# The last pair of heads of a fused transformer kernel: gates from exponentials, output chunks finished inside the loop, the last chunk in halves

## The reference, cut to what matters

```python
xn = layernorm(x)
s = attention1(xn)      # 16 heads of 64, causal, relative positions;
                        # s = concat(heads) @ out_kernel + out_bias
f = sigmoid(xr @ W_r.T) * (square(relu(xk @ W_k.T)) @ W_v.T)
g = f * sigmoid(f)      # silu
out = x + s * g
```

## Time and profile before

| what | value |
|---|---|
| median of three runs | 1199.7 us |
| the profiled execution's own time | 1197.8 us |
| its span in the trace | 1196.1 us |
| PE busy | 1138.2 us (95% of the span) |
| POOL busy | 832.8 us (70%) |
| DVE busy | 819.7 us (69%) |
| ACT busy | 688.4 us (58%) |

### The profile page before, as it was taken

The page is one execution under the profiler, slowest core; times in us unless marked ns, Lnnn a source line. Parts: engine busy times, 40 slices in busy tenths (PEclk is TensorE's granted clock), DMA queues, the critical chain, the costliest instruction groups (busy, mean ns, idle before and its releaser), DMA issues.

```text
span 1196.1 us, 31475 instructions
## 1 busy us (share of the span) xinstructions
PE 1138.2 (95%) x11940; PEld 751.9 (63%) x11948; DVE 819.7 (69%) x2041; ACT 688.4 (58%) x1376; POOL 832.8 (70%) x1111
## 2 busy tenths in 40 slices
PE   4999999999979999999999999999999999999997
PEld 1344566678736666667666766666676666676665
DVE  4778878613776876786687578668668767866552
ACT  3543363357335666576566656666666665765665
POOL 0787432102444987978888798788879879788895
PEclk9999999999999999999999999999999999999998
DMA  8300010113034220302302031040212203023001
GB/s 309 138 1 1 1 45 19 48 51 93 23 70 87 70 46 14 83 6 46 79 21 46 20 81 32 16 90 11 46 44 57 46 17 80 6 46 81 2 3 37
DMA packets 74891, 60.19 MB, mean 50 GB/s; under 512 B 38962, under 2 KB 69298, under 8 KB 73652
## 3 DMA queue, kind: packets, MB, share of 16 engines
q1 hardware_dynamic: 73716, 56.08, 18.8%
q0 software_dynamic: 1024, 2.09, 0.6%
HBM read 19.76 MB, written 4.72 MB: 20 GB/s over the span
## 4 chain that ended last, share of the span: by engine, by line
PE 68%; ACT 2%; DVE 1%; issue 1%; DVEq 0%
PE S L1980 10%; PE S L1981 10%; PE S L1982 10%; PE A L1970 9%; PE O L1994 6%; PE O L1995 5%; PE O L1992 5%; PE M L1961 3%; PE M L1938 2%; PE M L1940 2%; PE M L1939 2%; PE M L1955 1%; PE M L1948 1%; PE M L1946 1%; PE M L1947 1%
## 5 line engine op out<-in xcount | busy, mean ns | idle before, releaser
L1722 POOL TENSOR_TENSOR plow<-prob 128x512 f16<-128x512 f32 (+3 forms) x640 | 588.5, 931 | 94.5 <-ACT prob L2198 70.4
L2198 ACT ACTIVATE prob<-S,keep_sigma 128x512 f32<-128x512 f32 (+3 forms) x640 | 396.1, 626 | 263.7 <-PE S L1982 260.8
L2299 DVE CUSTOM_DVE_ANT_0 junk<-A,mask_rows,part 128x512 bf16<-128x512 f32 (+3 forms) x384 | 248.9, 648 | 98.0 <-PE A L1970 76.8
L1992 PE MATMUL O<-V,prob 128*128 128x65 f16 x2176 | 232.7, 193 | 0.2 <-POOL plow L1722 0.2
L1994 PE MATMUL O<-V,prob 128*128 128x64 f16 x2176 | 232.5, 194 | 0.0
L1995 PE MATMUL O<-V,plow 128*128 128x65 f16 x2176 | 231.7, 192 | 0.0
L1980 PE MATMUL S<-rows 97*128 97x512 f16 (+3 forms) x640 | 223.1, 349 | 3.8 <-ACT prob L2198 3.5
L1981 PE MATMUL S<-rows 96*128 96x512 f16 (+3 forms) x640 | 222.3, 347 | 0.0
L1970 PE MATMUL A<-rows 96*128 96x512 f16 (+3 forms) x640 | 221.0, 346 | 1.3 <-DVE part L2299 1.0
L1982 PE MATMUL S<-rows 96*128 96x512 f16 (+3 forms) x640 | 220.7, 345 | 0.0
L1992 PEld LDWEIGHTS O<-V,prob 128*128 128x128 bf16 x2176 | 203.0, 97 | 23.6 <-POOL plow L1722 0.3
(11 more groups left out here) (388 smaller groups left out, 1845.3 us busy)
## 6 DMA issues: line engine op xcount, KB each, us to landing
rows<-stage_rows SPq DMA_DIRECT2D x64, 256.0 KB, 3.4
V<-stage_v SPq DMA_DIRECT2D x16, 516.0 KB, 4.6
W<-in_W SPq DMA_DIRECT2D x2, 2048.0 KB, 14.2
shifted<-turned SPq DMA_DIRECT2D x32, 128.0 KB, 2.2
rows<-stage_pos SPq DMA_DIRECT2D x64, 64.0 KB, 3.1
w<-in_w SPq DMA_DIRECT2D x2, 1024.0 KB, 10.6
xe_rows<-zero SPq DMA_DIRECT2D x1, 1280.0 KB, 5.3
ye_rows<-xe SPq DMA_DIRECT2D x5, 256.0 KB, 3.2
```

Source lines behind the costliest of these rows:

```text
L1722: pool.tensor_tensor(plow[:, k % PB, 0:w], full, full.bitcast(BF16).rearrange("p (q e) -> p q e", e=2)[:, :, 1], ALU.subtract).then_inc(s_ ...
L1992: pe.matmul(both, high[:, cs, 1], vh[h][:, j, 0:HS + 1], start=(j == 0 and s == 0), stop=False, skip_group_check=True)
L2198: act.activation(prob[:, k % PB, 0:w], S[k % 2][:, 0:w], ACT.Exp, scale=sigma[:, 2 * p + h:2 * p + h + 1]).then_inc(s_exp, 1)
L2299: dve.tensor_tensor_reduce(junk[:, g % 2, 0:w], A[g % 2][:, 0:w], add, -1.0, before, ALU.add, ALU.min, out).then_inc(s_max, 1)
```

## The change

The gates are no longer made by Silu. In slots 22 to 29 of the last pair ACT writes exp(-f) into `turned`, in eight pieces of 256 columns (`negated`). DVE makes f / (1 + exp(-f)) from it with three operations for each chunk (`opened`), in slots 56, 60, 62 and 64. It multiplies `acc` by the gate and adds the residual (`finish`) for chunk 0 in slot 66, chunk 1 in 68, chunk 3 (without its last projection) in 73, and chunk 2 in 79. In a slot `opened` and `finish` stand behind the items and ahead of `inverted`. The last chunk of the last head sums its upper two tiles in bank A0 in place of O1, and is inverted, scaled, transposed, projected, multiplied by its gate, added and stored in two halves.

```diff
--- before.py
+++ after.py
@@ -1689,7 +1689,12 @@
         bank.n, bank.of_bank = 0, [0, 0]
         for _ in range(base_n + 7 * PER + TAIL):
             bank.take()
-        fin_items = [("turn", 0, 3, bank.take()), ("project", 0, 3, bank.take())]
+        HALF = TPC // 2
+        fin_turn = [bank.take() for _ in range(2)]
+        fin_project = [bank.take() for _ in range(2)]
+        NEGATED = {22 + k: k for k in range(2 * NC)}
+        OPENED = {56 + 2 * c + 2 * (c > 0): c for c in range(NC)}
+        FINISHED = {66: 0, 68: 1, 73: 3, 79: 2}
 
         JOINS = [(c, step) for c in range(NC) for step in range(3)]
         PRO_A = NB - LEAD
@@ -1828,11 +1833,12 @@
                 pair(p, False)
 
             pair(PAIRS - 1, True)
-            for c in range(NC):
-                sp.wait_ge(s_fin, 2 * c + 2)
-                sp.dma_start(out_dram.rearrange("b (n p) d -> p (b n) d", p=P)[:, TPC * c:TPC * (c + 1), :],
-                             acc[:, TPC * c:TPC * (c + 1), :]).then_inc(s_out, 16)
-            sp.wait_ge(s_out, 16 * NC)
+            stored = out_dram.rearrange("b (n p) d -> p (b n) d", p=P)
+            for ready, t0, t1 in ((2, 0, TPC), (4, TPC, 2 * TPC), (8, 2 * TPC, 3 * TPC), (10, 3 * TPC, 3 * TPC + HALF),
+                                  (12, 3 * TPC + HALF, NT)):
+                sp.wait_ge(s_fin, ready)
+                sp.dma_start(stored[:, t0:t1, :], acc[:, t0:t1, :]).then_inc(s_out, 16)
+            sp.wait_ge(s_out, 16 * 5)
 
 
         @block.gpsimd
@@ -1984,12 +1990,14 @@
 
             def values(h, c, j, n):
                 r = max(0, j - TPC * c)
+                halved = n >= ALL - TPC * NC
                 high = prob[:, n % PB, :].bitcast(BF16).rearrange("p (q e) -> p q e", e=2)
                 for s in range(r, TPC):
                     cs = slice((s - r) * P, (s - r + 1) * P)
                     at = s * (HS + 1)
-                    both, part = O[c % 2][:, at:at + HS + 1], O[c % 2][:, at:at + HS]
-                    pe.matmul(both, high[:, cs, 1], vh[h][:, j, 0:HS + 1], start=(j == 0 and s == 0), stop=False,
+                    sums = A[0] if halved and s >= HALF else O[c % 2]
+                    both, part = sums[:, at:at + HS + 1], sums[:, at:at + HS]
+                    pe.matmul(both, high[:, cs, 1], vh[h][:, j, 0:HS + 1], start=(j == 0 and (s == 0 or halved and s == HALF)), stop=False,
                               skip_group_check=True)
                     pe.matmul(part, high[:, cs, 1], vh[h][:, j, HS + 1:VW], start=False, stop=False, skip_group_check=True)
                     ins = pe.matmul(both, plow[:, n % PB, cs], vh[h][:, j, 0:HS + 1], start=False, stop=j == TPC * c + s,
@@ -2089,6 +2097,8 @@
                 if j == 0:
                     if 2 * NC * p + NC * h + c >= 2:
                         pe.wait_ge(s_otok, 2 * NC * p + NC * h + c)
+                    if 2 * NC * p + NC * h + c == 2 * NC * PAIRS - 1:
+                        pe.wait_ge(s_max, PRO_A + PER_A * (PAIRS - 1) + LEAD + NB)
                     if c == 0:
                         pe.wait_ge(s_mv[h], 16 * (p + 1))
                 pe.wait_ge(s_low, SLOTS * p + m + 1)
@@ -2104,9 +2114,20 @@
                 for k in two:
                     if k >= DRAIN:
                         value_tile(*divmod(k - DRAIN, SLOTS))
-            for (kind, rel, c, tok) in fin_items:
-                item(kind, rel, c, (tok[0] - PER * (PAIRS - 1), tok[1], tok[2] - PER // 2 * (PAIRS - 1)), PAIRS - 1,
-                     turn_tok=(fin_items[0][3][0], fin_items[0][3][1], fin_items[0][3][2] - PER // 2 * (PAIRS - 1)))
+            for k in range(2):
+                _, b, used = fin_turn[k]
+                pe.wait_ge(s_free[b], used)
+                pe.wait_ge(s_otok, 2 * NC * PAIRS + 1 + k)
+                for i in range(HALF * k, HALF * (k + 1)):
+                    ins = pe.transpose(M[b][:, i * P:(i + 1) * P], otok[:, TPC * (NC - 1) + i, :], ident[:])
+                ins.then_inc(s_item, 1)
+            for k in range(2):
+                pe.wait_ge(s_free[fin_turn[k][1]], fin_turn[k][2] + 1)
+                _, b, used = fin_project[k]
+                pe.wait_ge(s_free[b], used)
+                for i in range(HALF * k, HALF * (k + 1)):
+                    ins = pe.matmul(M[b][:, i * P:(i + 1) * P], oT[:, i * P:(i + 1) * P], wo[:, PAIRS, :], start=True, stop=True)
+                ins.then_inc(s_item, 1)
 
 
         @block.scalar
@@ -2207,12 +2228,33 @@
                     act.wait_ge(s_item, count(turn_item(plan[p == PAIRS - 1], -1, 3), p)[0])
                 if g == 0:
                     act.wait_ge(s_otok, 1)
+                if g == 2 * NC * PAIRS - 1:
+                    for k in range(2):
+                        act.wait_ge(s_rec, g + 1 + k)
+                        scaled_tiles(h, c, (O[c % 2], A[0])[k], HALF * k, HALF * (k + 1))
+                        _, b, _ = fin_turn[k]
+                        act.wait_ge(s_item, fin_turn[k][0] + 1)
+                        at = slice(HALF * k * P, HALF * (k + 1) * P)
+                        act.activation(oT[:, at], M[b][:, at], ACT.Copy).then_inc(s_free[b], 1)
+                    return
                 act.wait_ge(s_rec, g + 1)
-                for s in range(TPC):
+                scaled_tiles(h, c, O[c % 2], 0, TPC)
+
+            def scaled_tiles(h, c, sums, s0, s1):
+                for s in range(s0, s1):
                     ins = act.activation(otok[:, TPC * c + s, HS * h:HS * (h + 1)],
-                                         O[c % 2][:, s * (HS + 1):s * (HS + 1) + HS], ACT.Copy,
+                                         sums[:, s * (HS + 1):s * (HS + 1) + HS], ACT.Copy,
                                          scale=rsum[:, c % 2, s:s + 1])
                 ins.then_inc(s_otok, 1)
+
+            def negated(k):
+
+                if k == 0:
+                    act.wait_ge(s_gate, NC)
+                    act.wait_ge(s_psum, NC * PAIRS)
+                at = slice(k % 2 * (CW // 2), (k % 2 + 1) * (CW // 2))
+                g = gate[:, TPC * (k // 2):TPC * (k // 2 + 1), :].rearrange("p n d -> p (n d)")
+                act.activation(turned[:, k // 2, at], g[:, at], ACT.Exp, scale=-1.0).then_inc(s_silu, 1)
 
             for n in range(ALL + SCALE):
                 if n < ALL:
@@ -2220,16 +2262,10 @@
                     p, at = divmod(n, SLOTS)
                     for (kind, rel, c, tok) in plan[p == PAIRS - 1][at]:
                         item(kind, rel, c, tok, p, 0)
-                if n == ALL:
-                    act.wait_ge(s_gate, NC)
-                    for c in range(NC):
-                        at = gate[:, TPC * c:TPC * (c + 1), :]
-                        act.activation(at, at, ACT.Silu).then_inc(s_silu, 1)
+                    if p == PAIRS - 1 and at in NEGATED:
+                        negated(NEGATED[at])
                 if n >= SCALE:
                     scaled(*divmod(n - SCALE, SLOTS))
-            kind, rel, c, tok = fin_items[0]
-            act.wait_ge(s_item, tok[0] + 1)
-            act.activation(oT[:], M[tok[1]][:], ACT.Copy).then_inc(s_free[tok[1]], 1)
 
 
         @block.vector
@@ -2371,7 +2407,53 @@
                 if j == TPC * (c + 1) - 1:
                     dve.wait_ge(s_pv, SLOTS * p + m + 1)
                     sums = O[c % 2][:, 0:TPC * (HS + 1)].rearrange("p (s v) -> p s v", v=HS + 1)[:, :, HS]
+                    if SLOTS * p + m == ALL - 1:
+                        sums = A[0][:, 0:TPC * (HS + 1)].rearrange("p (s v) -> p s v", v=HS + 1)[:, :, HS]
+                        dve.reciprocal(rsum[:, c % 2, HALF:TPC], sums[:, HALF:TPC]).then_inc(s_rec, 1)
+                        return
                     dve.reciprocal(rsum[:, c % 2, :], sums).then_inc(s_rec, 1)
+                elif SLOTS * p + m == ALL - 3:
+                    dve.wait_ge(s_pv, ALL - 2)
+                    sums = O[c % 2][:, 0:TPC * (HS + 1)].rearrange("p (s v) -> p s v", v=HS + 1)[:, :, HS]
+                    dve.reciprocal(rsum[:, c % 2, 0:HALF], sums[:, 0:HALF]).then_inc(s_rec, 1)
+
+            def flat(x, c):
+                return x[:, TPC * c:TPC * (c + 1), :].rearrange("p n d -> p (n d)")
+
+            def opened(c):
+
+                e, g = turned[:, c, :], flat(gate, c)
+                dve.wait_ge(s_silu, 2 * c + 2)
+                step(dve.tensor_scalar(e, e, 1.0, None, ALU.add))
+                step(dve.reciprocal(e, e))
+                step(dve.tensor_tensor(g, g, e, ALU.mult))
+
+            fins = [0]
+
+            def finished(ins):
+                ins.then_inc(s_fin, 1)
+                fins[0] += 1
+
+            def finish(c):
+
+                kind, rel = ("project", -1) if c == NC - 1 else ("project", 0)
+                tok = next(x[3] for n in range(SLOTS) for x in plan[True][n] if x[:3] == (kind, rel, c))
+                dve.wait_ge(s_free[tok[1]], count(tok, PAIRS - 1)[2] + 1)
+                s = flat(acc, c)
```

(36 more changed lines are left out.)

## The result

The changed kernel took 1204.45 us as median of 8 runs, the kernel before 1199.38 us beside it: a ratio of 1.0038, 95% interval 1.0028 to 1.0048. It is slower by 0.38%, some 4.6 us. The forecast was 1203.9 us, slower, in a range of 1199.8 to 1207.6.

The account below looks back on a forecast made before the run. PE and POOL together bound the loop. A 6.4 us wait and 1.2 of clock move 1185.4 to 1193.0; a 7.3 tail gives 1200.3, 4.2 over 1196.1; added to median 1199.7: 1203.9 us, range 1199.8 to 1207.6.

Parts of the forecast that it names:

- The queue: DVE from slot 56: four openings, 18.4 us, delay slot 71's inversion, so ACT waits 6.4 us at its chunk 2 scaling.
- The exponentials: ACT, slots 22 to 29: eight exponentials of 256 columns, 3.8 us more work, taken as 0, upper end 1 us.
- Slot 60: Inversion for ACT's slot 60 behind the first opening: ready at 1163.5, against 1163.77 when ACT uses it; just fits.
- The clock: PE after ACT's wait: half speed over some 2.5 us of work costs 1.2 us, ends 0 and 2.5.
- POOL behind the wait: POOL around ACT's wait: no cost was added; POOL's losses were said to be made up while ACT waits.
- meetings: Openings' DVE operations beside POOL's splits: eight at 0.2 us cost DVE 1.6 us in all, ends 0 and 6.4.
- T: End of the last value product, when the sums are complete: forecast to move from 1185.4 to 1193.0.
- The tail: From the last value product to the end: 7.3 us in halves instead of 10.7, saving 3.4.
- The faster rival: DVE's wide reciprocal costs as a product, ACT never waits: 1197.8 us, or 1196.3 with POOL undisturbed; chance 0.15.
- threshold of 1.75 us: DVE's openings: ACT starts to wait when one opening costs over 1.75 us.
- The slower rival: DVE waits out a whole POOL split nearly every time, 6.4 us over eight operations: 1208.7 us; chance 0.10.

Follow-up runs that it names:

- both product runs: Kernel before plus 12 unread 128x512 products on DVE in slots 57 to 79: two SBUF inputs, ratio 1.0023; first input in PSUM, 1.0001.

## Why the prediction was right, and where its terms were off

- **The queue** was right in mechanism and size. A reciprocal of 512 columns took 3.35 us (3.4 forecast, from 16 and 64 columns). The inverse came 24.7 us after the last row maximum (24.6), and ACT waited 6.2 (6.4). Two doses show it: with reciprocals of 64 columns the wait is gone, with 2.8 us less work ahead it is 2.7 shorter. The eight operations of the openings took 2.3 us more than they take alone (1.6 forecast), and the rest of the list a little less.
- **The exponentials** in slots 22 to 29 were rightly put at 0. From the first exponential of `attention1` to the last row maximum it is 770.6 us before and after.
- **Slot 60.** "That just fits" did not: the first addition of a constant took 1.20 us in place of 0.45, beside a split. The inverse was ready 6.0 us after the last row maximum in place of 5.5, and every exponential from slot 61 on is 0.33 us late.
- **The clock** was a term too small: 1.2 forecast, for 2.5 us of work at half speed. PE had 5.34 us of work at a granted clock of 0.50, and keeping PE busy gave back 2.5 us (1.8 against the changed kernel run again). The prediction's own upper end was 2.5.
- **POOL behind the wait** had no term. The last meetings, with `finish` of chunk 2, come with 0.6 us of T that the exponentials don't explain (0.9 in the run again). No run takes these meetings alone away.
- **The tail** was a term too large: 7.3 against 6.0. About 0.7 of that is the clock: I priced the projection near the low one, and it ran at the high one, for which my own sum gives 6.6. The other 0.6 come from the start: the lower half's scaling ended 0.5 ahead of T (1196.39 against 1196.86) and not at T + 0.4, and the first projection at T + 2.1 and not at T + 2.75.

So T moved by 9.6 where 7.6 was forecast, and the tail gave 4.6 where 3.4 was. The two misses cancel in part: 5.0 us by the trace against 4.2. That the time fell within 0.6 us of the forecast is partly luck.

- **The faster rival** was rightly given a small chance, but its sum was wrong. It let a short reciprocal lead to 1197.8 us with 1.5 us for meetings. With short reciprocals in place the meetings cost 4.5 us, and the result was the time before. The step that failed was "I take 1.5 us" for sixteen meetings. Its threshold of 1.75 us has a small slip: it takes 9.6 us for the other work on DVE, and my own terms add up to 9.4; nothing hangs on it.
- **The slower rival.** A meeting at full price exists: where POOL had no gap, a product of 0.68 took 1.41 to 1.52 us. But of the eight operations ahead of the inversion only four waited, 0.33 to 0.75 us each, so they cost 2.3 us and not 6.4. The exclusive lock for a whole instruction that the Trainium skill describes (SBUF — State Buffer, SBUF: two separate sides) agrees with both product runs: 1235 ns from two SBUF inputs, 682 with one in PSUM.

Whether the first 1.8 us of the profiled execution have any cause in the change was not tried. The place of the first exponential differs between executions without any such cause: on the third chip it was 387.5 and 388.2 us in the two kernels with 12 products, and 388.0 and 391.7 in two forms of the changed one, whose edits all lie behind it.

## What to carry to other kernels

An engine that looks idle is a queue: before work is put on it, list what stands behind that work and when its reader wants it. Here one inversion of 0.18 us behind some 23 us of new work made ACT wait for 6.2 us, more than the 4.6 that the tail saved. Price wide operations by slope from narrow ones in the same trace, and keep VectorE operations with two SBUF inputs, or additions of a constant from SBUF to SBUF, away from a GpSimd without gaps; for a product, one input in PSUM was enough. When a wait is taken away, measure again before counting its gain, since it may have hidden a second cost.

## What was not expected of the hardware

- One input moved from SBUF to PSUM takes the whole contention away: 12 products at 682 ns against 1235, T unmoved against 3.5 us late.
- An addition of a constant from SBUF to SBUF meets POOL too: 0.45 us alone, 1.15 to 1.20 where a split was running.
- Tanh needed no table load between exponentials, where Silu needed one of 1.28 us.
- Behind a stretch of 5.8 us in which PE was busy for 1.31, the granted clock was 0.50 for 6.8 us and cost 2.5 us of the loop. 26 matmuls that nobody reads kept it at 1.00 and gave back 1.5 us at the end. The loss is not fixed: in the changed kernel run again it was 1.8.
